# The oldest convolution tap of the two x blocks: from one VectorE step to a ScalarE product and a GpSimd add

## What is computed

```python
xBC = zxbcdt[..., D_INNER:D_INNER + CONV_DIM]        # 512 channels: x (256), B (128), C (128)
xBC = conv_general_dilated(xBC, conv_w, padding=[(D_CONV - 1, 0)], groups=CONV_DIM)   # D_CONV = 4
xBC = xBC + conv_b
xBC = silu(xBC)
x_ssm, Bm, Cm = xBC[:256], xBC[256:384], xBC[384:]
# then the scan over tokens: h = dA*h + dt*x*B ; y = C.h + D*x
```

## Time and profile before

| | before |
|---|---|
| median of three runs | 817.68 us |
| the profiled execution: its time | 816.69 us |
| its span on the core | 814.9 us |
| TensorE matmuls busy | 667.5 us (82%) |
| VectorE busy | 617.5 us (76%) |
| ScalarE busy | 475.8 us (58%) |
| GpSimd busy | 433.0 us (53%) |
| entry and slots | 0 to about 460 us |
| experts and closing norm | about 480 us to the end |

### The profile page before, as it was taken

The page is one execution under the profiler, slowest core; times in us unless marked ns, Lnnn a source line. Parts: engine busy times, 40 slices in busy tenths (PEclk is TensorE's granted clock), DMA queues, the critical chain, the costliest instruction groups (busy, mean ns, idle before and its releaser), DMA issues.

```text
span 814.9 us, 21092 instructions
## 1 busy us (share of the span) xinstructions
PE 667.5 (82%) x5092; PEld 546.9 (67%) x5093; DVE 617.5 (76%) x2128; ACT 475.8 (58%) x1179; POOL 433.0 (53%) x498
## 2 busy tenths in 40 slices
PE   7969999888898898988987139999999999999300
PEld 5846666566665566655665129999999999999300
DVE  4398989889999899998896536666667666667485
ACT  3737766676766767667673115555555555556165
POOL 4023265656656566565756634555555555555464
PEclk9999999999999999999999559999999999999755
DMA  9160010111101111011100122222222222222496
GB/s 258 33 229 14 15 41 14 37 30 40 41 14 37 31 40 37 18 33 34 41 20 24 57 60 57 66 63 65 64 65 65 65 63 64 65 64 70 108 311 203
DMA packets 74801, 54.09 MB, mean 66 GB/s; under 512 B 9435, under 2 KB 70110, under 8 KB 74480
## 3 DMA queue, kind: packets, MB, share of 16 engines
q1 hardware_dynamic: 56400, 31.90, 14.9%
q0 software_dynamic: 8448, 16.93, 6.3%
q10 hardware_dynamic: 9888, 4.49, 2.0%
HBM read 31.11 MB, written 22.69 MB: 66 GB/s over the span
## 4 chain that ended last, share of the span: by engine, by line
PE 71%; issue 9%; ACT 7%; DVE 5%; POOL 3%; DMA 2%; ACTq 1%; SPq 1%; DVEq 0%; POOLq 0%
PE pl L633 16%; PE p L645 14%; PE pj L399 5%; PE p L585 4%; PE p L593 3%; PE p L542 3%; PE p L548 2%; PE pj L627 2%; ACT rowA L810 2%; ACT sz L872 2%; POOL sorted_rows L1366 2%; PE pj L407 2%; PE p L556 2%; PE p L496 2%; PE p L407 2%
## 5 line engine op out<-in xcount | busy, mean ns | idle before, releaser
L851 ACT ACTIVATE L<-pl,b_sb 128x128 f32<-128x128 f32 x544 | 155.4, 369 | 118.1 <-PE pl L633 118.1
L1428 POOL DMA_INDIRECT moe_rows<-yv,xs x136 | 145.7, 1072 | 140.5 <-DVE yv L1235 124.1
L633 PE MATMUL pl<-Btok,M 128*128 128x128 f32 x1088 | 151.7, 283 | 1.2 <-DVE M L1223 0.7
L924 DVE SCALAR_TENSOR_TENSOR acc<-pj,conv_w_sb,acc 128x511 f32<-128x511 f32 (+2 forms) x192 | 142.7, 743 | 4.0 <-ACT acc L730 1.1
L645 PE MATMUL p<-w,L 128*128 x1088 | 143.9, 275 | 1.3 <-ACT L L851 1.3
L633 PEld LDWEIGHTS pl<-Btok,M 128*128 128x128 f32 x1088 | 133.7, 193 | 4.3 <-DVE M L1223 1.4
L645 PEld LDWEIGHTS p<-w,L 128*128 128x128 f32 x1088 | 132.4, 192 | 1.8 <-issue 1.8
L1219 DVE COPY Btok<-pj 128x128 f32<-128x128 f32 x136 | 39.7, 292 | 78.2 <-PE pl L633 63.2
L1379 POOL TENSOR_TENSOR Xdd<-Xdt,cur 128x256 f32<-128x256 f32 x48 | 29.5, 615 | 88.0 <-DVE Xdt L1091 80.1
L1366 POOL DMA_INDIRECT sorted_rows<-rowA,slot x64 | 64.7, 1011 | 19.1 <-issue 17.0
L1366 POOL DMA_INDIRECT sorted_rows<-rowB,slot x64 | 62.7, 980 | 18.0 <-issue 18.0
(11 more groups left out here) (204 smaller groups left out, 1341.7 us busy)
## 6 DMA issues: line engine op xcount, KB each, us to landing
xs<-sorted_rows SPq DMA_DIRECT2D x136, 65.0 KB, 1.8
xres<-in_x SPq DMA_DIRECT2D x16, 256.0 KB
w<-in_w SPq DMA_DIRECT2D x2, 2048.0 KB, 10.2
acc<-moe_rows SPq DMA_DIRECT2D x16, 256.0 KB, 4.2
xc<-moe_rows SPq DMA_DIRECT2D x16, 256.0 KB, 5.0
out<-sz ACTq DMA_DIRECT2D x16, 256.0 KB, 4.6
moe_rows<-yv,xs POOLq DMA_INDIRECT x136, 2.4
xc<-in_x SPq DMA_DIRECT2D x4, 256.0 KB, 5.1
```

What stands on the lines that cost most here:

```text
L633: mm = pe.matmul(pl[k % 2][:, f * P:(f + 1) * P], w1e[k % 2][:, f * P:(f + 1) * P], sT[k % 2][:, :], start=True, stop=True)
L851: act.activation(hT[k % 2][:, f, :], pl[k % 2][:, f * P:(f + 1) * P], ACT.Gelu, bias=b1[:, bass.ds(e * FB + f, 1)]).then_inc(hT_ready, 1)
L924: ins = dve.scalar_tensor_tensor(out=acc[:, k, j:TOKS], in0=pj[k % 2][:, 0:TOKS - j], scalar=conv_w[:, k, TAPS - 1 - j:TAPS - j], in1=acc[ ...
L1428: pool.indirect_dma_start(out=moe_rows[:, :], out_offset=bass.IndirectOffsetOnAxis(xs[k][:, P:P + 1].bitcast(I32), 0), in_=ye[k % 4], in_o ...
```

## The change

Blocks 0 and 1 (`BY_POOL = 2`) lose their last VectorE tap. In its place ScalarE multiplies the oldest tap out of the PSUM bank into a new buffer `oldest[k]`, straight behind `tap0` of the block, and GpSimd adds that buffer to `acc`. The add of block 0 is put behind gt 1, the add of block 1 behind gt 2. The first VectorE tap of these blocks also waits for the product, so that the bank is free once VectorE is through; the counter is now called `taps_read`, and the Silu of blocks 0 and 1 waits for the add.

```diff
@@ tensor
-                    wait(pe, conv_done, XC * q.n + k - 1)
+                    wait(pe, taps_read, XC * q.n + k - 1)
@@ scalar
                 act.activation(acc[:, c, :], pj[c % 2][:, :], ACT.Identity, bias=conv_b[:, c:c + 1],
                                scale=conv_w[:, c, TAPS - 1:TAPS]).then_inc(tap0_done, 1)
+                if c < BY_POOL:
+                    wait(act, oldest_added, BY_POOL * (q.n - 1) + c + 1)
+                    act.activation(oldest[c][:, TAPS - 1:TOKS], pj[c % 2][:, 0:TOKS - TAPS + 1], ACT.Identity,
+                                   scale=conv_w[:, c, 0:1]).then_inc(tap3_done, 1)
 
             def activate(q, k):
-                act.wait_ge(conv_done, XC * q.n + k + 1)
+                if k < BY_POOL:
+                    act.wait_ge(oldest_added, BY_POOL * q.n + k + 1)
+                else:
+                    act.wait_ge(taps_read, XC * q.n + k + 1)
@@ vector
+                on_dve = TAPS - 1 - (k < BY_POOL)
+                if j > on_dve:
+                    return
...
                 if j == 1:
                     dve.wait_ge(tap0_done, XC * q.n + k + 1)
+                    if k < BY_POOL:
+                        dve.wait_ge(tap3_done, BY_POOL * q.n + k + 1)
@@ gpsimd
+            def add_oldest(q, k):
+                pool.wait_ge(tap3_done, BY_POOL * q.n + k + 1)
+                pool.wait_ge(taps_read, XC * q.n + k + 1)
+                pool.tensor_tensor(acc[:, k, TAPS - 1:TOKS], acc[:, k, TAPS - 1:TOKS], oldest[k][:, TAPS - 1:TOKS],
+                                   ALU.add).then_inc(oldest_added, 1)
...
                     gate_y(s, 1)
+                if project:
+                    add_oldest(q, 0)
                 if scatters:
                     scatter(old, 0, 0)
                     scatter(old, 1, 0)
                 if scan:
                     gate_y(s, 2)
+                if project:
+                    add_oldest(q, 1)
```

More of the change, by code:

```diff
@@ L49 @@
 G0 = 2
+BY_POOL = 2
 Q = 32
@@ L127, in build @@
         acc = sb("acc", [P, XC, TOKS])
+        oldest = [sb(f"oldest{i}", [P, TOKS]) for i in range(BY_POOL)]
         xc = [sb(f"xc{i}", [P, XC, TOKS]) for i in range(2)]
@@ L242, in build @@
          state_psum, ss_psum, out_psum, uT_psum, logit_psum, rank_psum, S_psum) = [sem(n) for n in names_pe]
-        names_act = ("xT_ready", "abs_done", "ev_ready", "L_ready", "tap0_done", "Btok_ready", "sq_done", "cur_ready", "S_ready",
+        names_act = ("xT_ready", "abs_done", "ev_ready", "L_ready", "tap0_done", "tap3_done", "Btok_ready", "sq_done", "cur_ready", "S_ready",
                      "uT_ready", "rowB_ready", "eg_ready", "decays_ready", "xc_ready", "sz_ready",
                      "xD_ready")
-        (xT_ready, abs_done, ev_ready, L_ready, tap0_done, Btok_ready, sq_done, cur_ready, S_ready, uT_ready, rowB_ready,
+        (xT_ready, abs_done, ev_ready, L_ready, tap0_done, tap3_done, Btok_ready, sq_done, cur_ready, S_ready, uT_ready, rowB_ready,
          eg_ready, decays_ready, xc_ready, sz_ready, xD_ready) = [sem(n) for n in names_act]
         names_dve = ("x1_ready", "Gm_ready", "M_ready", "Xdt_ready", "v_ready", "yv_ready", "state_ready",
-                     "sp_step", "a_ready", "tap_done", "conv_done", "carried_ready", "ln_step", "ve_ready", "shift_ready",
+                     "sp_step", "a_ready", "tap_done", "taps_read", "carried_ready", "ln_step", "ve_ready", "shift_ready",
                      "u_ready", "gate_step", "chosen_ready", "ms_ready", "pos_step", "rank_read",
@@ L252, in build @@
         (x1_ready, Gm_ready, M_ready, Xdt_ready, v_ready, yv_ready, state_ready, sp_step, a_ready,
-         tap_done, conv_done, carried_ready, ln_step, ve_ready, shift_ready, u_ready, gate_step, chosen_ready,
+         tap_done, taps_read, carried_ready, ln_step, ve_ready, shift_ready, u_ready, gate_step, chosen_ready,
          ms_ready, pos_step, rank_read, slot_ready, parts_ready, split_step) = [sem(n) for n in names_dve]
-        names_pool = ("picks_made", "Xdd_ready", "decayed_ready", "g_ready", "rms_ready", "rstd_ready")
-        (picks_made, Xdd_ready, decayed_ready, g_ready, rms_ready, rstd_ready) = [sem(n) for n in names_pool]
+        names_pool = ("oldest_added", "picks_made", "Xdd_ready", "decayed_ready", "g_ready", "rms_ready", "rstd_ready")
+        (oldest_added, picks_made, Xdd_ready, decayed_ready, g_ready, rms_ready, rstd_ready) = [sem(n) for n in names_pool]
         scattered = [[sem(f"scattered_{'AB'[k]}{i}") for k in range(2)] for i in range(2)]
@@ L405, in z_block @@
                 else:
-                    pe.wait_ge(conv_done, XC * q.n + 3)
+                    pe.wait_ge(taps_read, XC * q.n + 3)
                 pe.matmul((pj[0], p6)[k][:, :], w_z[:, k * P:(k + 1) * P], xT[:, q.n, :],
@@ L917, in tap @@
             def tap(q, k, j):
-                done = (TAPS - 2) * (XC * q.n + k)
+                on_dve = TAPS - 1 - (k < BY_POOL)
+                if j > on_dve:
+                    return
+                done = (XC * (TAPS - 2) - BY_POOL) * q.n + (TAPS - 2) * k - min(k, BY_POOL)
                 if j == 1:
                     dve.wait_ge(tap0_done, XC * q.n + k + 1)
+                    if k < BY_POOL:
+                        dve.wait_ge(tap3_done, BY_POOL * q.n + k + 1)
                 else:
@@ L927, in tap @@
                     op0=ALU.mult, op1=ALU.add)
-                if j < TAPS - 1:
+                if j < on_dve:
                     ins.then_inc(tap_done, 1)
                 else:
-                    ins.then_inc(conv_done, 1)
+                    ins.then_inc(taps_read, 1)
             def enter_dt(g, lo, hi):
@@ L1387, in slot_pool @@
                     make_picks()
+                    for k in range(BY_POOL):
+                        add_oldest(q, k)
                     return
```

## The result

| | before, same chip | after |
|---|---|---|
| median | 817.27 us (4 runs, 816.50 to 819.04) | 844.83 us (4 runs, 843.28 to 845.88) |
| ratio, 95% interval | | 1.0333 [1.0309, 1.0356] |
| profiled execution; its span | 816.69; 814.9 us | 844.97; 843.1 us |
| matmuls busy | 667.5 us | 685.3 us |
| VectorE, ScalarE, GpSimd busy | 617.5, 475.8, 433.0 us | 600.2, 493.4, 472.9 us |

The change costs 3.3%. The forecast was 837.0 with a range to 846: right in sign and in its range, 7.8 us short. The page of the kernel after gives the busy times. TensorE, which got no new instruction, is busy 17.8 us longer; that is the first sign of something that the sum did not hold.

What follows compares the result with a forecast made beforehand. The bound was taken to be a chain through `S`, TensorE and GpSimd's queue, not VectorE. Slots 2 to 13 +18.5, slot 14 +1.0, slot 1 +0.6, entry +0.6, slot 0 -1.3: +19.4, forecast 837.0 us, range 827 to 846.

Steps and rivals of the forecast that it cites:

- VectorE's taps are not on the path in slots 1 to 14: Removing two VectorE taps a slot there gains nothing, since TensorE and ScalarE set the time in chunks 1 and 2.
- Slot 0, -1.3 us: In slot 0 the chain runs through VectorE's taps, so removing two saves 2 x 0.67 us, once.
- The product ahead of `S`, +0.60 us a slot: Block 1's ScalarE product stands between `tap0` and `S`, where TensorE waits: +0.6 us in each of slots 1 to 14.
- Slot 1, +0.6: Slot 1 has no scatters, so the adds are hidden and only +0.6 us is added.
- In the entry I forecast +0.6: Before the slots, both products precede the copy of the third transposed input; the second adds +0.6 us.
- The adds: 1.29 us: Each GpSimd add of 128 x 509 takes 1.29 us, from similar rows; ends 0.94 and 1.47 us.
- The projection late by 1.88: Each slot's output projection starts 1.88 us late: gt 3 ends 3.18 us later, less 1.3 us of cover.
- The state update's wait shrank, as forecast: TensorE's wait of 1.32 us for `Xdd` ahead of L556 gets smaller, as `Xdd` moves by only 1.0 us.
- Per slot 1.54: In slots 2 to 13 each period grows 1.54 us: 1.88 less 0.34 us of wait at `state`; ScalarE's step included.
- 0.6 + 18.5 + 1.0 = 20.1: Slots 1 to 14: slot 1 +0.6, slots 2 to 13 12 x 1.54 = +18.5, slot 14 +1.0 us, where `Xdd` decides.
- Its upper end, 844.2 rounded up to 846: Slow end of the same sum: adds of 1.47, products of 0.77, per slot 2.07 us, giving 844.2; range to 846.
- Rival 3: Adds and VectorE taps hold each other up, 1.5 us in each of 13 slots, +19.5: 856.5 us; chance 0.07.

Runs made afterwards that it cites:

- experiment 4: Kernel before, with the oldest tap of blocks 0 and 1 left out of the computation, no product and no add: 815.83 us, ratio 0.9986.
- experiment 2: Changed kernel, with the add of block 0 moved ahead of the `Xdd` of chunk 2 and that of block 1 behind gt 3: 840.79 us.
- experiment 5: Kernel before, plus a ScalarE product of block 1 that nothing reads, ahead of `tap0`, `cur` and `S` in chunk 1: 840.80 us.
- experiment 7: Changed kernel, plus six matmuls that nothing reads, inside TensorE's wait for `S` in chunk 1: 837.10 us.
- experiment 1: Changed kernel, with the ScalarE product of block 1 moved behind the copies `cur` and `S`: 826.61 us.
- experiment 3: Changed kernel, with the product of block 1 behind `S`, add 0 ahead of the `Xdd` of chunk 2 and add 1 behind gt 3: 819.29 us.
- experiment 11: Changed kernel, with `S` ahead of the layer norm, block 1's product behind it, adds in GpSimd's gaps, two `rowB` scatters in the next slot's gap: 825.99 us.
- experiment 12: Kernel of experiment 11, with the add of block 0 put back behind gt 1, beside VectorE's taps: 813.88 us.

## Why the prediction came out as it did

- **VectorE's taps are not on the path in slots 1 to 14: right**, shown by experiment 4.
- **Slot 0, -1.3 us: wrong in sign, measured +1.25.** The taps' gain is real (-1.5 in experiment 4). The step that failed is that I let the adds there cost nothing; moved into GpSimd's gaps (experiment 2) they leave the slot 1.8 us shorter. Slot 0 has work of its own on VectorE, the softplus, with all operands in SBUF. It stretches while GpSimd adds; in the trace of after a 2.4 us wait of TensorE and a half-clock spell follow. What each of the two is worth there was not separated.
- **The product ahead of `S`, +0.60 us a slot: right**, measured 0.57 as a step and as a period (experiment 5). Slot 1, +0.6: right, the copies of `S` around it are 0.56 further apart in experiment 7. In the entry I forecast +0.6, and the first inner product came at 38.55 in place of 38.52: nothing.
- **The adds: 1.29 us right (1.27)**. The 1.12 us worked out from the Trainium skill ("GPSIMD Engine Reference", section 3.1) was too short for it. The projection late by 1.88: about right, as `S` is 0.6 late and the wait for gt 3 is 1.1 (14.5 us in 13 times in experiment 7, where no spell disturbs it), 1.7 in all. The state update's wait shrank, as forecast.
- **Per slot 1.54: measured 1.33**, 0.57 (experiment 5) and 0.75 (experiment 1) when made apart. Over slots 1 to 14 (forecast 0.6 + 18.5 + 1.0 = 20.1) the trace has 383.43 us, from 68.59 to 452.02, against 357.62: +25.8. Six spells of 1.22 are 7.3 of it, the other 18.5 are 14 x 1.32. The terms were 1.6 too large.
- **The missing term is the half-clock spells.** With slot 0 they make the difference: 18.5 + 7.3 + 1.25 = 27.1; slot 15 gives 0.9 back, and 2.0 come behind it, in the experts, that the forecast called untouched. They go with the clock too: before the experts the granted clock is at 0.50 for a while in every kernel, and it ends 32.4 us behind the last transposes of the norm in the kernel before (486.7 us) and 36.7 us in the one after (517.2). In the 14 traces the rest of the program takes 359.9 to 360.9 us where that time is 32.5 us or less and 361.6 to 362.7 where it is 36.0 or more. What sets it was not tried. The forecast priced each wait by its length. It took TensorE's clock for given, 1.00 in the earlier trace rows, and never asked what a longer wait does to the matmuls behind it.
- **That the measured time lies in the range is luck.** Its upper end, 844.2 rounded up to 846, stood for adds of 1.47 us and products of 0.77. They took 1.27 and 0.68, and the time got there by spells that the sum doesn't hold; without them (experiment 7) it is 837.1.
- **Rival 3**, VectorE and GpSimd holding each other up, was rejected for the taps, rightly: in every kernel they stay near 750 ns. Its mechanism exists, though, and decides elsewhere. I looked for it only at the instructions that the change names, and not at the others that the adds run beside. The rule of the Trainium skill ("SBUF — State Buffer", section "SBUF: two separate sides"), that a VectorE instruction with two SBUF inputs and a GpSimd instruction lock each other out for a whole instruction, fits the 1.24 us above. The instruction of 1.96 us has one tensor input, and no run here shows by which part of the rule it is held.

That mechanism is at work in the kernel before as well, on the path that the forecast names. `shift`, with which the chain leaves VectorE, has two SBUF inputs and takes 0.46 us in each of slots 2 to 14; it ends with GpSimd's `Xdd`, and the layer norm waits for it. At 452.38 us, with GpSimd idle, it takes 0.16.

```profile
201.03 0.61 POOL L1379 TENSOR_TENSOR Xdd<-Xdt,cur 128x256 f32<-128x256 f32 x1 [0.90 <-DVE Xdt L1091]
201.20 0.46 DVE L1103 SCALAR_TENSOR_TENSOR shift<-mv,rstd 128x4 f32<-128x4 f32 x1
201.70 1.65 ACT L810 ACTIVATE rowA<-rowA,shift,rstd 128x128 f32<-128x128 f32 x4 [1.26 <-DVE shift L1103]
```

So some 0.3 us a slot of the path through `S` may be this hold, an estimate from these rows; no run took it out.

By the two profiled executions the span grew 28.2 us where the sum had 19.4. The 8.8 between them: spells 7.3, slot 0 2.6, behind the slots 2.0, less 1.6 in the steps, 0.9 in slot 15 and 0.6 in the entry.

## What to carry to other kernels

An engine at 90% busy can still be off the path: take its work away alone and see, before paying for that with work on the engines that the path goes through. Price a step ahead of a long wait of TensorE by more than its own length: where one 0.6 us product lengthened a wait from 1.5 to 2.1 us, the slower clock behind the wait cost about as much again in the change (7.3 us beside 14 x 0.57) and twice as much in experiment 5. If work goes to GpSimd, place it beside VectorE instructions that read PSUM, and read the durations of all small instructions that it runs beside, not only of those that were moved.

## What the runs showed of the hardware

- TensorE's granted clock fell to 0.50 behind waits of 2.1 us in some slots, for some 3.4 us, and cost 1.2 us each in the change and 1.6 in experiments 2 and 5. Behind waits of 1.5 us in slots 2 to 14 of experiments 1 and 3 it did not. But 2.1 us is no border: it also fell behind 1.76 us (experiment 11) and 1.60 us (experiment 4). Matmuls that nothing reads, put into the wait, made the kernel 7.7 us faster. Why some of these waits bring a spell and others of the same length don't stays open.
- GpSimd held up some VectorE instructions with all operands in SBUF: 0.153 to 1.24 us beside one add, 0.158 to 1.96 beside two instructions. Not all: in the kernel before the reduction `slotf` (128x64 to 128x8) ran its 0.22 us beside `decayed` 14 times and ended 0.24 us ahead of it. An indirect DMA issued by GpSimd seems to do it too: in experiment 12 the 0.63 us of `rowB` end with one (203.43 beside 203.40). Yet `rowA<-top,gsum`, the same kind of instruction, ran its 0.17 us beside the same DMA from 202.66 on and was not held. That was not tested by itself.
- A GpSimd add of 128 x 509 took 1.27 us with two different inputs, written into one of them, and 1.04 us with one tensor as both inputs and another as output. An imitation of a cost must copy the operands too.
